# Splitting W_V and W_O in their own layout and turning them by the transfer queue, in a layer-norm and linear-attention kernel

## What is computed

```
norm(x) = (x - mean) / sqrt(var + 1e-5)      # over the 512 numbers of a token
ffn(t)  = norm(t + outs) * ln_g + ln_b       # outs: an attention over gathered tokens
attn(x): q, k, v = x @ Wq.T, x @ Wk.T, x @ Wv.T      # 16 heads of 32
         phi_q, phi_k = elu(q) + 1, elu(k) + 1
         for each token: S = S + phi_k (outer) v;  z = z + phi_k
                         o = (phi_q @ S) / (phi_q . z + EPS)
         return o @ Wo.T + bo
x = x + 0.5 * ffn(norm(x))
x = x + attn(norm(x))
x = x + 0.5 * ffn(norm(x))
```

## Time and profile before

| | us |
|---|---|
| median of 3 runs | 940.27 |
| lowest, highest | 939.8, 940.8 |
| the profiled execution | 940.58 |
| its span | 938.8 |
| TensorE busy | 898.5 (96%) |
| VectorE busy | 827.4 (88%) |
| ScalarE busy | 758.4 (81%) |
| GpSimd busy | 711.6 (76%) |

### The profile page before, as it was taken

The page is one execution under the profiler, slowest core; times in us unless marked ns, Lnnn a source line. Parts: engine busy times, 40 slices in busy tenths (PEclk is TensorE's granted clock), DMA queues, the critical chain, the costliest instruction groups (busy, mean ns, idle before and its releaser), DMA issues. The chain is left out here.

```text
span 938.8 us, 29969 instructions
## 1 busy us (share of the span) xinstructions
PE 898.5 (96%) x10252; PEld 525.8 (56%) x10252; DVE 827.4 (88%) x1531; ACT 758.4 (81%) x1327; POOL 711.6 (76%) x875
## 2 busy tenths in 40 slices
PE   3899999999999999999999999999999999999974
PEld 2455556555555655555565555556565555655542
DVE  6888899999999999999999999999999999998764
ACT  5978788888888888888888888888888888888861
POOL 2277787788777788878778987777898777779761
PEclk9999999999999999999999999999999999999986
DMA  8286887866687666768767666876766787776762
GB/s 290 41 174 123 171 159 156 138 153 151 144 179 156 149 142 148 151 148 179 156 146 144 146 151 151 179 156 141 146 149 148 154 171 161 144 121 128 128 118 68
DMA packets 421405, 139.81 MB, mean 149 GB/s; under 512 B 402544, under 2 KB 402544, under 8 KB 421360
## 3 DMA queue, kind: packets, MB, share of 16 engines
q1 hardware_dynamic: 404496, 106.73, 60.5%
q10 hardware_dynamic: 16864, 32.51, 10.6%
HBM read 21.76 MB, written 16.78 MB: 41 GB/s over the span
## 5 line engine op out<-in xcount | busy, mean ns | idle before, releaser
L1302 PE MATMUL PJ<-wT,XT 128*128 128x512 f16 x2304 | 525.1, 379 | 1.7 <-DMA XT<-XH 1.4
L1302 PEld LDWEIGHTS PJ<-wT,XT 128*128 128x128 f16 x2304 | 216.6, 98 | 245.3 <-DMA XT<-XH 3.2
L459 POOL TENSOR_TENSOR A<-AM,A 128x512 f16<-128x512 f32 x256 | 292.5, 1162 | 35.4 <-ACT A L677 35.4
L1401 PE MATMUL PJ<-wT,AT 128*128 128x512 f16 x768 | 178.6, 383 | 1.2 <-DMA AT<-ATTN 1.2
L451 POOL TENSOR_SCALAR_AFFINE_SELECT AM<-AM 128x512 f32<-128x512 f32 x128 | 82.0, 641 | 113.1 <-ACT AM L667 113.1
L677 ACT ACTIVATE A<-AM 128x512 f16<-128x512 f32 x256 | 154.0, 630 | 12.6 <-POOL AM L451 11.3
L1372 PE MATMUL AV<-SS,QS 128*128 128x33 f16 x1024 | 112.3, 178 | 4.9 <-POOL A L459 4.4
L1375 PE MATMUL AV<-VN,A 128*128 128x33 f16 x3072 | 116.9, 178 | 0.0
L1401 PEld LDWEIGHTS PJ<-wT,AT 128*128 128x128 f16 x768 | 71.6, 98 | 79.8 <-issue 2.7
L1375 PEld LDWEIGHTS AV<-VN,A 128*128 128x128 f16 x3072 | 109.3, 96 | 3.7
L992 DVE TENSOR_TENSOR AM<-SC,causal 128x512 f32<-128x512 f32 x128 | 87.5, 684 | 22.9 <-PE SC L1352 22.9
(11 more groups left out here) (101 smaller groups left out, 1531.8 us busy)
## 6 DMA issues: line engine op xcount, KB each, us to landing
out_dram<-Y ACTq DMA_DIRECT2D x32, 512.0 KB, 3.1
X<-in_L_attn_x_dram ACTq DMA_DIRECT2D x30, 512.0 KB, 3.5
X<-in_L_attn_x_dram SPq DMA_DIRECT2D x2, 512.0 KB, 8.0
A<-in_L_attn_Wk_dram SPq DMA_DIRECT2D x1, 1024.0 KB, 8.3
A<-in_L_attn_Wq_dram SPq DMA_DIRECT2D x1, 1024.0 KB, 10.5
QS<-in_L_attn_Wv_dram SPq DMA_DIRECT2D x1, 1024.0 KB, 12.7
QS<-in_L_attn_Wo_dram SPq DMA_DIRECT2D x1, 1024.0 KB, 16.0
XT<-XH SPq DMA_TRANSPOSE x64, 3.4
```

The source lines that it names most:

```text
L459: g.tensor_tensor(A[:, b, LO, hg], AM[:, k % 4], A[:, b, HI, hg], ALU.subtract).then_inc(a_lo.sem, 1)
L1302: ins = t_.matmul(PJ[b], XT[:, w, c, b * C:(b + 1) * C], wT[m_][:, m, c, :], start=(c, w, m) == todo[0], stop=(c, w, m) == todo[-1])
L1401: ins = t_.matmul(PJ[b], AT[:, b, w, c * C:(c + 1) * C], wT[3][:, m, c, :], start=(c, w, m) == todo[0], stop=(c, w, m) == todo[-1])
```

## The change

W_K and W_Q stay as they were. W_V and W_O are split before they are turned. ScalarE writes the high half straight from `wnat` in the weight's own layout (`w_half` for j of 2 and 3), GpSimd scales the same rows into AM and subtracts the high half (`w_low` on GpSimd), both into `staged`, which lies where W_K and W_Q were loaded, once those are turned. The sync queue then turns each of four row groups by one transposing transfer of 8 blocks (`turn_w`), straight to `wT`. TensorE loses 32 transposes, VectorE eight `w_low`. There are new waits: for TensorE on the turned weights (`w_turned`), and for ScalarE's first `split_a` of each batch, since its tile A is where the halves were staged. The openings of all five engines stand in a new order. The bodies are untouched.

```diff
+        staged = [None, None] + [A[:, 1 - m].rearrange("p f g q -> p (f g q)").rearrange("p (o f e) -> p o f e", o=GROUPS, f=2)
+                                 for m in range(2)]
...
-        W_BANKS = PJ + [spare[k % 3] for k in range(4 * GROUPS - 2)]
+        W_BANKS = PJ + [spare[k % 3] for k in range(2 * GROUPS - 2)]
...
+            def turn_w(j, o):
+                m = W_ORDER[j]
+                sp.wait_ge(w_split, (j - 2) * GROUPS + o + 1)
+                sp.dma_start_transpose(wT[m][:, :, :, o * P:(o + 1) * P].rearrange("p f c q -> p (f c) q"),
+                                       staged[m][:, o].rearrange("p f e -> p (f e)")).then_inc(w_turned[m], 16)
...
-                            sp.wait_ge(wT_hi, (4 if ATTEND else 3) * GROUPS)
+                            sp.wait_ge(w_split, (2 if ATTEND else 1) * GROUPS)
                         sp.wait_ge(*q_lo.upto(n, b))
...
+            def w_low(j, c):
+                m = W_ORDER[j]
+                pool.wait_ge(w_scaled, j + 1)
+                link(g.tensor_scalar(AM[:, c], wnat[m][:, c], w_scale[:, m:m + 1], None, ALU.mult))
+                pool.wait_ge(wT_hi, j * GROUPS + c + 1)
+                g.tensor_tensor(staged[m][:, c, LO], AM[:, c], staged[m][:, c, HI], ALU.subtract).then_inc(w_split, 1)
...
                 act.wait_ge(w_scaled, j + 1)
-                act.wait_ge(wT_filled, k + 1)
-                a.activation(wT[m][:, HI, c], W_BANKS[k][:], ACT.Copy, scale=w_scale[:, m:m + 1]).then_inc(wT_hi, 1)
+                if j < 2:
+                    act.wait_ge(wT_filled, k + 1)
+                    to, w = wT[m][:, HI, c], W_BANKS[k][:]
+                else:
+                    act.wait_ge(wT_filled, (4 - j) * GROUPS)
+                    to, w = staged[m][:, c, HI], wnat[m][:, c]
+                a.activation(to, w, ACT.Copy, scale=w_scale[:, m:m + 1]).then_inc(wT_hi, 1)
...
-                        if hg == 0 and FINISH:
-
+                        if hg == 0 and not FINISH:
+                            act.wait_ge(w_turned[3 - b], GROUPS * 16)
+                        elif hg == 0:
                             act.wait_ge(*av_filled.upto(back, 2 * b + 1))
...
-                half_gain()
                 early.front_stats(0)
                 early.front_stats(1)
+                half_gain()
...
-                            pe.wait_ge(wT_lo, 3 * GROUPS)
+                            pe.wait_ge(w_turned[2], GROUPS * 16)
                         pe.wait_ge(*q_lo.upto(n, b))
                         project(2, b, v_filled)
...
-                                pe.wait_ge(wT_lo, 4 * GROUPS)
+                                pe.wait_ge(wT_lo, 2 * GROUPS)
...
+                        if not FINISH and b == 0:
+                            pe.wait_ge(w_turned[3], GROUPS * 16)
```

More of the change, by code:

```diff
@@ L166, in build @@
         wT_lo = sem("wT_lo")
+        w_split = sem("w_split")
+        w_turned = [sem(f"w_turned{m}") for m in range(4)]
         gain_scaled = sem("gain_scaled")
@@ L348, in opening @@
                 early.turn_x(1)
+                turn_w(2, 0)
+                turn_w(2, 1)
+                turn_w(2, 2)
+                turn_w(2, 3)
+                turn_w(3, 0)
+                first.turn_k(0)
+                turn_w(3, 1)
                 first.turn_q(0)
[L350 removed]
                 first.turn_x(0)
+                turn_w(3, 2)
+                turn_w(3, 3)
+                first.turn_x(1)
                 first.turn_q(1)
[L353 removed]
                 first.turn_k(1)
@@ L782, in opening @@
-                w_half(1, 0)
+                square(2, 1)
+                w_half(1, 0)
+                early.normalise(0)
+                square(2, 2)
+                early.x_half(0)
+                square(2, 3)
+                early.normalise(1)
                 w_half(1, 1)
                 w_half(1, 2)
+                w_half(1, 3)
+                early.x_half(1)
+                square(3, 0)
+                w_half(2, 0)
+                square(3, 1)
+                w_half(2, 1)
                 first.front_scale(0)
+                square(3, 2)
@@ L807, in opening @@
-                first.q_half(1)
+                second.front_scale(0)
                 first.x_half(1)
                 first.v_half(0)
-                first.next_x()
-                w_half(3, 1)
-                w_half(3, 2)
-                w_half(3, 3)
                 first.v_half(1)
-                second.front_scale(0)
+                second.copy_scores(0, 1)
+                second.split_a(0, 0)
                 second.front_scale(1)
-                second.split_a(0, 0)
-                second.copy_scores(0, 1)
+                second.copy_scores(0, 3)
```

158 lines of the change are left out of this document (70 added, 88 removed).

## The result

| | before | after |
|---|---|---|
| time, median (lowest to highest) | 940.53 (939.80 to 941.52), 4 runs | 952.57 (951.32 to 952.77), 4 runs |
| ratio, 95% interval | | 1.0118 (1.0099 to 1.0138) |
| span of the profiled execution | 938.8 | 950.9 |
| v(1) starts, takes | 47.18, 2.75 | 53.12, 5.01 |
| mark: scores(1, 2) of chunk 0 starts | 62.25 | 70.79 |

The account below looks back on a forecast made before the run. TensorE, 96% busy, was taken as the bound, waiting only in the opening behind ScalarE. 0.0 - 0.94 - 0.7 + 0.3 = -1.34 us took the profiled 940.58 to 939.2, against the median 938.9; range 936.6 to 941.9.

Parts of the forecast that it names:

- Start: Opening up to the first projections: front_scale at 8.1 instead of 9.34 us; k(0) then at 28.9 instead of 24.27.
- GpSimd: the step that failed: GpSimd's opening: scaling 0.64 us, each split 1.9, rstd1 at 42.1, just ahead of normalise(0) on ScalarE.
- if the scaling takes over 0.9: Stated sign that the forecast is wrong: GpSimd's scaling, expected at 0.64 us, takes over 0.9.
- the third rival: GpSimd becomes the bound: scaling 1.16 us, split 2.4, slower from about 2.2; 941.5 to 945 us, chance 0.14.
- Its slack is gone but it is not late: GpSimd's opening: it reaches split_a(0, 0) at about 52.5 us as before, now without idling.
- the first term, 0.0: k(0) to v(1): the later start is just paid for, v(1) ends at 49.9 us against 49.93; 0.0.
- Second and third term: scores(0, 0) no longer waits for a low half, -0.94 us; second k(1) waits 0.3 instead of 0.99, -0.7.
- The fourth term: scores(1, 0) waits for the turned k, landing 4.5 us after issue: +0.3 us, between 0 and 0.6.
- a second rival: TensorE stays slow in k(0) and k(1), adding 0.8 to 2 us: 939.7 to 940.9, chance 0.16 with smaller latenesses.
- The middle carries it to the end: After the mark the long middle is unchanged, so the mark's gain of 1.34 us arrives whole at the end.
- my -1.3: Sum of the four terms at the mark, -1.34 us: 60.9 instead of 62.25.

Follow-up runs that it names:

- e1: The changed kernel with the low halves of W_V and W_O made by VectorE in one instruction each, none by GpSimd: 945.9 us, ratio 1.0054.
- e2: The changed kernel with GpSimd's scaling left out, so the low halves are not right: 946.2 us, one run.
- e3: The changed kernel with GpSimd's scaling as a two-input operation against the broadcast scale: 947.3 us, ratio 1.0056.
- e16: The changed kernel without GpSimd's scaling (low halves not right) and with both x loads behind the copy of scores(1, 1): 942.4 us, ratio 1.0012.
- e9: The changed kernel with both x loads of ScalarE's opening moved behind the copy of scores(1, 1): 948.4 us, ratio 1.0070.
- e18: The kernel before the change with its two x loads of the opening moved beside the turned k: 946.2 us, ratio 1.0048.
- e8: The changed kernel with 24 matmuls more on TensorE between v(0) and v(1): 954.0 us, one run.
- e12: The kernel before the change with x's statistics ahead of halving the gain and the next x load ahead of the first square: 941.3 us, ratio 0.9993.

## Why the prediction was wrong, step by step

- *Start.* front_scale ran at 8.75, forecast 8.1 (9.34 before): the gain landed at 6.76 instead of 6.14. k(0) at 29.39 for 28.9, and 4.93 us for 4.3; k(1) at 35.11 for 34.3. 0.8 us, a size.
- **GpSimd: the step that failed.** "I take 0.64, since one tensor is read", within a bound of 0.64 to 1.16: it took 1.56. By my own sign ("if the scaling takes over 0.9") the forecast was wrong here. The upper bound was not one: the nearest rows were other operations, and I took the count of inputs for the price. rstd1 came at 48.1 for 42.1, v(1) started 6.0 us late and took 2.3 more. Its own mechanism was in the third rival, which asked for a split of 2.2 us to be slower than before; the split was 2.8, which the rival reaches only with a hold of 0.45 in every split (2.85, by its own sum +5.6), and its 941.5 to 945 left that out. The holds did not come: one scaling of eight took 2.00 instead of 1.56; the price itself was the higher one. "Its slack is gone but it is not late" was the warning: a chain without reserve, costed at the lowest end. e1, e2 and e3 give back 6.1, 5.0 and 3.4 us of the mark.
- **So the first term, 0.0, was +8.2**: v(1) ends at 58.13 (53.12 + 5.01) for 49.93. With -1.1 at scores(0, 0), -1.0 at the second k(1) and +2.5 at scores(1, 0) that makes 8.6, and the mark moved by 8.54. GpSimd is most of the 8.2, but not all: without its scaling v(1) still starts at 49.1 and 49.2 (e2, e16), where I had 47.1. Of these 2 us, 1.0 (after) to 1.7 (e16) stand at the end of q(0) already, 40.5 and 41.2 for 39.5: the late start, and the slow clock in k(0).
- *Second and third term* came as forecast: scores(0, 0) follows v(1) without a wait, and so does the second k(1).
- **The fourth term failed by itself.** "It lands 4.5 later" was the median of 64 turns, whose slowest had taken 7.1, and that one had a load of x beside it: the row to price from was there. I had walked SP's queue but not the transfers that ScalarE issues: I left out `first.next_x()`, which the change sets beside `second.next_x()` and the turned k. +2.52 where I had +0.3. e9 and e18 show it from both sides.
- *The slow clock at v(1)*, a second rival at another place, was real (5.01 us) and cost nothing at the mark (e8), because the turned k came later still. At the second q(1), behind the mark, it costs 1.3 of the 3.56 us: TensorE is 8.54 late at the mark and 9.9 late at the first output projection.
- **"The middle carries it to the end" failed in size.** The stretch behind the mark grew by 3.56 us: 1.3 at the second q(1), and 2.6 of waits for XT and AT between 139 and 207 us, after which the distance to the kernel before no longer grows (12.5 at 225 us, 12.4 at 636). From the mark to the end it is 876.6 us before, 880.1 after, 877.2 in e1, 877.6 in e12, 876.4 in e18, but 880.5 in e9 and 878.5 in e16. It goes with none of the edits alone. That the moment at which the steps are entered decides which transfer is late in them is a guess, and why these turns come late stays open.
- *What remains* with both wrong terms gone (e16, +1.2 us in time, +0.2 at the mark, although k(0) started 5.8 later than before): v(1) ends at 51.98, 2.0 later than before, and most of this is covered because of the waits of 0.94 and 0.99 behind it the first is gone and the second is 0.47. So the first term's zero was 2 us short even there, and that the mark is nearly as before owes something to luck. Whether my -1.3 could be had is not shown: in e16 a score still waits 1.19 for a turn that the late loads hold up. The walk on TensorE, ScalarE and VectorE held within 1 us up to q(0) in the kernel after, and was 2 us short at v(1); further off I was on the two resources that I priced by their nearest or typical row.

## What to carry to other kernels

An operation that the trace does not show is not bounded by rows of other operations, even of the same shape and engine: where an engine's slack is used up to the last, forecast with the dear end, and ask what happens beyond it. When instructions are reordered, walk every queue that issues transfers: loads of 512 KB beside a turn that someone waits for made that turn 1 to 6 us later here, though they are on different queues. Look, too, at what stands beside the slowest row of a group before pricing from its median. And taking work from TensorE in a stretch where it waits for others gives back only waits that this very work had caused: here the 0.94 us for W_O's last low half.
